# Inverse deviations and exponentials as powers on GpSimd instead of Sqrt and Exp on ScalarE

## The chip, the cores and the metric

One core of a Trainium2 chip runs the whole program. The metric is the device time of one execution in microseconds; the profile adds a span, from the first to the last instruction. The engines are TensorE (PE), VectorE (DVE), ScalarE (ACT), GpSimd (POOL) and SyncE (SP); each works through its own queue in order, and they meet through semaphores.

## The reference

The input x is 32 images of 64 channels, 16 x 16 pixels, fp32. Two blocks with residuals are computed. The second one, which the change touches, is a layer norm over 64 channels, a softmax router over 8 experts with the top two kept, and a mixture of expert networks:

```python
x = x + _L0_conv_ref(_ln_c(x), L0_conv_w)          # fake-quantised 3x3 convolution
t = _to_tokens(x)
t = t + _L0_ffn_ref(_ln_t(t), gate_w, gate_b, W1, b1, W2, b2)

def _ln_t(v, eps=1e-05):
    return (v - mean(v)) / sqrt(var(v) + eps)

logits = xf @ gate_w + gate_b
probs = softmax(logits)
top2_vals, top2_idx = top_k(probs, 2)              # cw: these two values at their experts, else 0
# over the 8 experts:
h = gelu(xf @ w1 + bb1);  y = h @ w2 + bb2;  acc = acc + cw_e * y
```

## The kernel before

The 32 images are handled as 16 pairs: two images of 64 channels fill the 128 partitions, and their 4096 columns are cut into 8 chunks of W = 512. A chunk holds 1024 tokens, as 8 groups of 128 (GROUPS). The order of work on every engine is written out by hand; an engine runs its queue in order.

Stage 1 (to about 35 us) is the first norm and the fake quantisation of its result. Stage 2 (35 to 57 us): TensorE convolves chunk c (convolve, L885), and two chunks behind subtracts the channel means of the new x by a product with a centering matrix (center_x2). GpSimd writes each quantised chunk into a padded tile (quantised, L337) and adds the residual of chunks 0 to 4 (residual, L345); its queue is quantised(0), (1), (2), residual(0), quantised(3), residual(1), then for c = 4, 5, 6 quantised(c) and residual(c-2), and quantised(7).

The second norm: ScalarE squares the centered chunk (square, L386), VectorE sums by group (reduce_squares, L563), ScalarE takes sqrt(sum/64 + eps) for a part of several chunks (deviations, L391), VectorE inverts it (invert, L569) and multiplies (normalise, L575). The parts are chunks 0-1, 2-3 and 4-7 (LN2_PARTS): 16, 16 and 32 columns for a partition.

The router: TensorE transposes the normalised chunk (transpose_x2), a copy brings it to SBUF (take_xT), and TensorE takes the logits. VectorE adds the bias, takes the maximum over experts and subtracts it (shifted_logits, L688, semaphore z_ready). ScalarE takes exponentials in place in ex (exponentials, L455, semaphore exp_ready); the parts are again chunks 0-1, 2-3 and 4-7 (LOGIT_PARTS), 128, 128 and 256 columns. For each chunk VectorE then finds the top two: route_copy (L703, to lcur), route_max, route_index, route_sum (L723, waits for exp_ready), route_select, and route_gates (L733), which multiplies exponentials, selection and inverse sum. TensorE transposes the gates (transpose_gates, L933), ScalarE copies them (take_gateT), and SyncE writes them to DRAM and reads them back spread over the partitions (spread_gates, L250).

Stage 3 (69 us to the end) is the expert networks, 8 units (experts) for each of 8 chunks. A unit is first_product (L947, weights times tokens), Gelu on ScalarE (gelus, L487), second_product (L960), weigh on VectorE (L744: bias, times gate, into y_sb, a ring of 4 tiles), and add_unit on GpSimd (L363: add y to x2). TensorE's first product may run two units ahead of the Gelu; second_product(n) waits for weighted >= n-1, and weigh(n) waits until add_unit(n-4) is done. Inside ffn on VectorE (L757) the router of chunk c+2 is spread between the weigh steps; in ffn(0) shifted_logits(2) stands after weigh(0,3), and route_gates(2) after weigh(0,4).

ScalarE holds one table of functions at a time. Square and Copy need no load of their own in this trace; the loads are for Sqrt (start), Exp (L459, twice) and Gelu (L500 and L504, each a dummy activation that draws the load forward). exponentials(2) stands after the 8 Gelus of chunk 0.

Of the kernel before, what the change touches and what calls it, by code (L numbers as in the profile page):

```python
# [3 lines left out]


IMAGES, CH, SIDE = 32, 64, 16
PIX = SIDE * SIDE
EXPERTS, HIDDEN = 8, 128
TAPS = 9
PAIRS = IMAGES // 2  # L10
NCH = 8
# [3 lines left out]
GROUPS = 2 * TILES  # L15
# [5 lines left out]
LN1_EPS, LN2_EPS = 1e-6, 1e-5  # L21
# [25 lines left out]
def program(nc, x, conv_w, gate_w, gate_b, W1, b1, W2, b2, out):  # L47
# [15 lines left out]
    with ctx:  # L63
        def sb(name, shape, dt=fp32):
            return ctx.enter_context(nc.sbuf_tensor(name, shape, dt))
# [15 lines left out]

        logit = sb("logit", [128, NCH, GROUPS, EXPERTS])
        lmax = sb("lmax", [128, NCH, GROUPS])
        ex = sb("ex", [128, NCH, GROUPS, EXPERTS])
        lcur = sb("lcur", [128, GROUPS, EXPERTS])
        top = sb("top", [128, GROUPS, 8])
        topi = sb("topi", [128, GROUPS, 8], u32)
# [93 lines left out]
        ss2 = sem("ss2")  # L181
# [102 lines left out]
        def _(pool):  # L284
            count = [0]

            def link(ins):
                count[0] += 1
                ins.then_inc(pool_link, 1)
                pool.wait_ge(pool_link, count[0])  # L290
# [3 lines left out]

            pool.memset(center[:, :], 0.0)
            pool.memset(gate_bd[:, :, :], 0.0).then_inc(gatebd_zero, 1)
            link(pool.memset(identf[:, :], 0.0))
            pool.memset(center[0:CH, 0:CH], -1.0 / CH)
            link(pool.memset(center[CH:128, CH:128], -1.0 / CH))
# [37 lines left out]
            def quantised(c):  # L337

                wait_alone(pool, (biased_ready, c + 1))
                pool.tensor_tensor(qpad[:, ds(2 * c, 2), 1:SIDE + 1, 1:SIDE + 1],  # L340
                                   work[:, ds(c * W, W)].rearrange("p (q h w) -> p q h w", q=2, h=SIDE),
                                   xn[:, ds(c * W, W)].rearrange("p (q h w) -> p q h w", q=2, h=SIDE),
                                   ALU.subtract).then_inc(q_ready, 1)

            def residual(c):  # L345

                wait_alone(pool, (conv_taken, c + 1))
                pool.tensor_tensor(x2[:, ds(c * W, W)], x2[:, ds(c * W, W)], x_sb[:, ds(c * W, W)],  # L348
                                   ALU.add).then_inc(x2_ready, 1)

            quantised(0)
            quantised(1)
            quantised(2)
# [1 line left out]
            quantised(3)  # L355
            residual(1)

            with pool.Fori(4, NCH - 1) as c:
                quantised(c)
                residual(c - 2)  # L360
            quantised(NCH - 1)

            def add_unit(c, u):  # L363
                n = UNITS * c + u
# [7 lines left out]

            for u in range(UNITS):
                add_unit(0, u)
            with pool.Fori(1, NCH - 1) as c:
                for u in range(UNITS):
                    add_unit(c, u)
# [5 lines left out]
        def _(act):  # L383
# [68 lines left out]
                act.wait_ge(x2T_ready, c + 1)  # L452
                act.activation(xT[:, ds(c * W, W)], bank(c), ACT.Copy).then_inc(xT_by_act, 1)  # L453

            def exponentials(k):  # L455

                first, last = LOGIT_PARTS[k]
                act.wait_ge(z_ready, k + 1)
                act.activation(ex[:, first:last, :, :], ex[:, first:last, :, :], ACT.Exp).then_inc(exp_ready, 1)  # L459

            def take_gateT(c):

                act.wait_ge(gateT_done, c + 1)
# [4 lines left out]
                               ACT.Copy).then_inc(gateT_ready, 1)  # L468


            deviations(LN2_PARTS[0], ss2, eps2, std2)
            square(3, cent2, sq2)
            deviations(LN2_PARTS[1], ss2, eps2, std2)
            square(4, cent2, sq2)
            square(5, cent2, sq2)
            take_xT(0)
            square(6, cent2, sq2)
            take_xT(1)
            square(7, cent2, sq2)
            deviations(LN2_PARTS[2], ss2, eps2, std2)  # L480
            exponentials(0)
            take_xT(2)
            take_xT(3)
            take_gateT(0)
            exponentials(1)

            def gelus(c, gates_after=2):  # L487
                for u in range(UNITS):
# [10 lines left out]

            act.activation(std[:, 0, 0:1], eps1[:, 0:1], ACT.Gelu)  # L500
            gelus(0, gates_after=3)
            exponentials(2)

            act.activation(std[:, 0, 0:1], eps1[:, 0:1], ACT.Gelu)  # L504
            with act.Fori(1, NCH - 1) as c:
                gelus(c)
            gelus(NCH - 1, gates_after=None)
# [2 lines left out]
        def _(dve):  # L510
# [177 lines left out]
            def shifted_logits(k):  # L688

                first, last = LOGIT_PARTS[k]  # L690
                n = (last - first) * GROUPS
                at = logits_at(first)
                dve.wait_ge(logits_done, last)
                l = logit[:, first:last, :, :].rearrange("p z g e -> p (z g) e")
                link(dve.tensor_tensor(l, ps[:, at:at + n * EXPERTS].rearrange("p (g e) -> p g e", e=EXPERTS),
                                       gb_sb[:, :].unsqueeze(1).to_broadcast([128, n, EXPERTS]), ALU.add))
                m = lmax[:, first:last, :].rearrange("p z g -> p (z g)")
                link(dve.tensor_reduce(m, l, AX.X, ALU.max))
                dve.tensor_tensor(ex[:, first:last, :, :].rearrange("p z g e -> p (z g) e"), l,
                                  m.unsqueeze(2).to_broadcast([128, n, EXPERTS]), ALU.subtract).then_inc(z_ready, 1)  # L700


# [74 lines left out]

            reduce_squares(2, sq2, ss2)
            residual(5)
            invert(LN2_PARTS, 0, std2, rstd2)  # L780
            normalise(0, LN2_PARTS, rstd2, xn2_ready)
            normalise(1, LN2_PARTS, rstd2, xn2_ready)
            reduce_squares(3, sq2, ss2)
            residual(6)
            invert(LN2_PARTS, 1, std2, rstd2)
            normalise(2, LN2_PARTS, rstd2, xn2_ready)
            normalise(3, LN2_PARTS, rstd2, xn2_ready)
            residual(7)
# [5 lines left out]
            shifted_logits(0)  # L794
            settled()
            route_copy(0)
            invert(LN2_PARTS, 2, std2, rstd2)
            route_max(range(GROUPS))
            normalise(4, LN2_PARTS, rstd2, xn2_ready)
            route_index(range(GROUPS))  # L800
# [231 lines left out]
```

## Time and profile before

| | us |
|---|---|
| median of 3 runs | 219.78 |
| their lowest and highest | 218.99, 220.37 |
| the profiled execution | 218.63 |
| its span, first to last instruction | 216.7 |

| engine | busy us | share of the span |
|---|---|---|
| PE (matmul) | 188.4 | 87% |
| DVE | 137.1 | 63% |
| POOL | 115.5 | 53% |
| ACT | 104.8 | 48% |

Busy shares are averages over three stages of different kinds. A matmul's end is modelled, so TensorE's share says that it seldom lacks work and not that it is at its peak. A bracket at the end of a row, as [0.28 <-ACT work L494], gives the engine's idle time just before the instruction and what ended it. TensorE's granted clock is a share of full speed: 1.00 is 2.4 GHz, 0.50 is 1.2 GHz.

### The profile page before, as it was taken

To read this page: it belongs to the slowest core of one execution; us is meant where nothing else is said; L and a number is where in the kernel's file an instruction comes from. 1 tells how busy PE (TensorE), PEld (TensorE's weight loads), DVE (VectorE), ACT (ScalarE), POOL (GpSimd) and SP (SyncE) were. 2 spreads that over 40 slices of the span, in tenths; PEclk is the share of its full clock that TensorE was granted. 3 is DMA by queue.
4 is the path that set the end of the run, shared out by engine and by line. 5 is a ranking of instruction groups with operands and counts; after the bars stand their busy time and mean duration, and the time that the engine had idled before them with its cause. 6 is when DMAs were issued, how large, how long until landed. Compare 5 with 4: busy or idle time off the path is not lost.

```text
span 216.7 us, 3237 instructions
## 1 busy us (share of the span) xinstructions
PE 188.4 (87%) x859; PEld 73.1 (34%) x859; DVE 137.1 (63%) x436; ACT 104.8 (48%) x140; POOL 115.5 (53%) x108
## 2 busy tenths in 40 slices
PE   2966105999979989999999999999999999999990
PEld 2954101566766335422222222222222222222220
DVE  0999999996759655754754664663773763334342
ACT  2539700333372724396465555645555465554640
POOL 7696007799000024456565665756656565665663
PEclk9999755999995899999999999999999999999998
DMA  6940000000000593970890890693692593495101
GB/s 175 316 71 3 0 2 0 0 3 0 3 0 1 142 201 79 202 166 7 209 224 11 203 213 28 152 204 88 166 206 67 143 207 91 124 200 120 50 0 48
DMA packets 16176, 22.36 MB, mean 103 GB/s; under 512 B 2202, under 2 KB 7970, under 8 KB 16162
## 3 DMA queue, kind: packets, MB, share of 16 engines
q1 hardware_dynamic: 16002, 22.04, 45.0%
q8 instruction: 7, 0.11, 0.2%
q10 hardware_dynamic: 160, 0.15, 0.2%
q14 instruction: 7, 0.06, 0.1%
HBM read 19.82 MB, written 2.36 MB: 102 GB/s over the span
## 4 chain that ended last, share of the span: by engine, by line
PE 74%; DVE 14%; issue 4%; DMA 2%; ACT 2%; POOL 1%; POOLq 1%; DVEq 1%; ACTq 0%
PE ps L956 30%; PE ps L971 27%; PE ps L889 8%; PE ps L846 3%; PE ps L929 3%; DVE ssum L566 2%; DVE xn L578 2%; DMA cw<-in_conv_w 2%; PE ps L916 2%; DVE topi L715 1%; DVE gbc L613 1%; PE ps L944 1%; DVE xn L617 1%; DVE cw_x L601 1%; DVE cw_max L539 1%
## 5 line engine op out<-in xcount | busy, mean ns | idle before, releaser
L370 POOL TENSOR_TENSOR x<-x,y_sb 128x512 f32 (+1 forms) x63 | 80.2, 1272 | 79.2 <-DVE y_sb L754 79.1
L494 ACT ACTIVATE work<-ps,bias_sb 128x1024 f32<-128x1024 f32 x64 | 71.2, 1114 | 62.9 <-PE ps L956 62.9
L754 DVE SCALAR_TENSOR_TENSOR y_sb<-ps,bias_sb,gbc 128x512 f32<-128x512 f32 x64 | 48.0, 750 | 59.4 <-PE ps L971 56.5
L956 PE MATMUL ps<-xT,w_sb 64*128 64x512 f32 x256 | 73.4, 650 | 0.1
L971 PE MATMUL ps<-work,w_sb 128*64 128x512 f32 x256 | 68.8, 617 | 0.1
L956 PEld LDWEIGHTS ps<-xT,w_sb 64*128 64x128 f32 x256 | 19.6, 188 | 43.4 <-issue 42.4
L971 PEld LDWEIGHTS ps<-work,w_sb 128*64 128x64 f32 x256 | 12.8, 134 | 48.5 <-issue 37.7
L889 PE MATMUL ps<-qpad,cw_bd 128*128 128x512 bf16 x72 | 18.6, 410 | 10.2 <-POOL qpad L340 10.2
L340 POOL TENSOR_TENSOR qpad<-work,xn 128x512 bf16<-128x512 f32 (+1 forms) x8 | 11.1, 1401 | 7.4 <-issue 7.4
L389 ACT ACTIVATE work<-ps 128x512 f32<-128x512 f32 x16 | 9.3, 596 | 10.9 <-PE ps L846 10.9
L889 PEld LDWEIGHTS ps<-qpad,cw_bd 128*128 128x128 bf16 x72 | 7.2, 101 | 19.4 <-issue 12.6
L846 PE MATMUL ps<-center,x_sb 128*128 128x128 f32 x64 | 9.1, 313 | 3.8 <-DMA x_sb<-in_x 3.8
L566 DVE TENSOR_REDUCE ssum<-work 128x8 f32<-128x512 f32 x16 | 10.5, 678 | 2.6 <-ACT work L389 2.6
L442 ACT ACTIVATE x<-ps 128x512 f32<-128x512 f32 x5 | 3.0, 599 | 18.2 <-PE ps L889 18.2
L929 PE MATMUL ps<-gate_bd,xT 128*128 128x16 f32 x64 | 9.0, 284 | 1.4 <-ACT xT L453 1.4
L846 PEld LDWEIGHTS ps<-center,x_sb 128*128 128x128 f32 x64 | 8.9, 228 | 3.8 <-POOL stack_id L306 3.8
L929 PEld LDWEIGHTS ps<-gate_bd,xT 128*128 128x128 f32 x64 | 8.7, 218 | 3.3 <-ACT xT L453 1.7
L578 DVE TENSOR_TENSOR xn<-ps,rstd 128x512 f32<-128x512 f32 x14 | 9.2, 682 | 0.1
L715 DVE FIND_INDEX8 topi<-top,lcur 128x8 uint32<-128x8 f32 x64 | 8.9, 159 | 0.0
L348 POOL TENSOR_TENSOR x<-x,x_sb (+1 forms) x5 | 7.8, 1564 | 1.6 <-ACT x L442 1.6
L846 PEld LDWEIGHTS ps<-center,x 128*128 128x128 f32 x64 | 8.2, 191 | 1.0
L846 PE MATMUL ps<-center,x 128*128 128x128 f32 x64 | 8.4, 275 | 0.0
(88 smaller groups left out, 140.3 us busy)
## 6 DMA issues: line engine op xcount, KB each, us to landing
gbc<-gate_rows SPq DMA_DIRECT2D x16, 768.0 KB, 9.7
gbc<-gate_rows SPq DMA_DIRECT2D x16, 256.0 KB, 4.1
x_sb<-in_x SPq DMA_DIRECT2D x8, 256.0 KB, 5.5
out<-x SPq DMA_DIRECT2D x8, 256.0 KB, 9.7
w_sb<-in_W SPq DMA_DIRECT2D x3, 256.0 KB, 6.9
gate_rows<-gateT SPq DMA_DIRECT2D x8, 32.0 KB, 1.9
cw<-in_conv_w ACTq DMA_DIRECT2D x2, 72.0 KB, 3.7
gate_bd<-in_gate_w SPq DMA_DIRECT2D x2, 2.0 KB, 6.1
```

What stands on the lines that cost most here:

```text
L340: pool.tensor_tensor(qpad[:, ds(2 * c, 2), 1:SIDE + 1, 1:SIDE + 1], work[:, ds(c * W, W)].rearrange("p (q h w) -> p q h w", q=2, h=SIDE), ...
L370: pool.tensor_tensor(x2[:, ds(c * W, W)], x2[:, ds(c * W, W)], y_sb[:, u % H_RING, :], ALU.add).then_inc(added, 1)
L494: act.activation(h_sb[:, u % H_RING, :], bank(H + 2 * (u % 2), 2 * W), ACT.Gelu, bias=b1_sb[:, u:u + 1]).then_inc(gelu_done, 1)
L566: dve.tensor_reduce(ssum[:, ds(c, 1), :].rearrange("p z g -> p (z g)"), by_group(work[:, ds(c * W, W)]), AX.X, ALU.add).then_inc(summed, 1)
L578: dve.tensor_tensor(by_group(xn[:, ds(c * W, W)]), by_group(bank(c)), wide_groups(rstd, c), ALU.mult).then_inc(ready, 1)
L715: last = dve.max_index(topi[:, g, :], top[:, g, :], lcur[:, g, :])
L754: dve.scalar_tensor_tensor(y_sb[:, u % H_RING, :], bank(Y + u % 2), b2_sb[:, u:u + 1], gbc[:, slot, u, :], ALU.add, ALU.mult).then_inc(wei ...
L846: last = pe.matmul(ps[:, col:col + 128], src[:, col:col + 128], center[:, :], start=True, stop=True)
L889: last = pe.matmul(bank(c), cw_bd[:, k, :, :].rearrange("p r o -> p (r o)"), qpad[:, ds(2 * c, 2), k // 3:k // 3 + SIDE, k % 3:k % 3 + SID ...
L929: last = pe.matmul(by_image[:, :, t, :], xT[:, c * W + t * 128:c * W + (t + 1) * 128], gate_bd[:, :, :], start=True, stop=True)
L956: last = pe.matmul(bank(H + 2 * (u % 2) + r), w1_sb[r * CH:(r + 1) * CH, u * HIDDEN:(u + 1) * HIDDEN], xT[r * CH:(r + 1) * CH, ds(c * W, W ...
L971: last = pe.matmul(ps[r * CH:(r + 1) * CH, (Y + u % 2) * W:(Y + u % 2 + 1) * W], w2_sb[:, u, :], h_sb[:, u % H_RING, r * W:(r + 1) * W], s ...
```

## The change

The Sqrt activations of the second norm and VectorE's three reciprocals behind them are replaced by (ssum/64 + eps) to the power -0.5 on GpSimd: one tensor_scalar and one tensor_tensor with the operation pow. The router's Exp becomes e to the power z, one tensor_tensor on GpSimd for each part; VectorE writes the shifted logits into a new tile z instead of ex. Two constant tiles are filled at the start (256 and 32 columns). GpSimd's loop over c = 4 to 6 is written out, so that inverse_deviations(0) can stand between residual(3) and quantised(6). inverse_deviations(1) and (2) and exponentials(0) and (1) follow quantised(7); exponentials(2) stands after add_unit(0,3). ScalarE loses the Exp table loads and the second Gelu load with its dummy.

```diff
@@ gpsimd
+            pool.memset(euler[:, :], math.e)
+            pool.memset(neg_half[:, :], -0.5)
...
+            def inverse_deviations(k):
+                first, last = LN2_PARTS[k]
+                n = (last - first) * GROUPS
+                wait_alone(pool, (ss2, last))
+                link(pool.tensor_scalar(std[:, first:last, :], ssum[:, first:last, :], 1.0 / CH, LN2_EPS,
+                                        ALU.mult, ALU.add))
+                pool.tensor_tensor(rstd[:, first:last, :].rearrange("p z g -> p (z g)"),
+                                   std[:, first:last, :].rearrange("p z g -> p (z g)"),
+                                   neg_half[:, 0:n], ALU.pow).then_inc(rstd2, 1)
+            def exponentials(k):
+                first, last = LOGIT_PARTS[k]
+                n = (last - first) * GROUPS * EXPERTS
+                wait_alone(pool, (z_ready, k + 1))
+                pool.tensor_tensor(ex[:, first:last, :, :].rearrange("p z g e -> p (z g e)"), euler[:, 0:n],
+                                   z[:, first:last, :, :].rearrange("p z g e -> p (z g e)"),
+                                   ALU.pow).then_inc(exp_ready, 1)
...
-            with pool.Fori(4, NCH - 1) as c:
+            for c in range(4, NCH - 1):
                 quantised(c)
                 residual(c - 2)
+                if c == 5:
+                    inverse_deviations(0)
             quantised(NCH - 1)
+            inverse_deviations(1)
+            inverse_deviations(2)
+            exponentials(0)
+            exponentials(1)
...
             for u in range(UNITS):
                 add_unit(0, u)
+                if u == 3:
+                    exponentials(2)
@@ scalar
-            deviations(LN2_PARTS[0], ss2, eps2, std2)
             square(3, cent2, sq2)
-            deviations(LN2_PARTS[1], ss2, eps2, std2)
...
-            deviations(LN2_PARTS[2], ss2, eps2, std2)
-            exponentials(0)
             take_xT(2)
             take_xT(3)
             take_gateT(0)
-            exponentials(1)
...
             act.activation(std[:, 0, 0:1], eps1[:, 0:1], ACT.Gelu)
             gelus(0, gates_after=3)
-            exponentials(2)
-
-            act.activation(std[:, 0, 0:1], eps1[:, 0:1], ACT.Gelu)
@@ vector
-                dve.tensor_tensor(ex[:, first:last, :, :].rearrange("p z g e -> p (z g) e"), l,
+                dve.tensor_tensor(z[:, first:last, :, :].rearrange("p z g e -> p (z g) e"), l,
...
-            invert(LN2_PARTS, 0, std2, rstd2)
...
-            invert(LN2_PARTS, 1, std2, rstd2)
...
-            invert(LN2_PARTS, 2, std2, rstd2)
```

## Rows read from the trace of the kernel before

**Rows 1.** The page's head and its first part: span, busy time by engine.
```profile
span 216.7 us, 3237 instructions
PE 188.4 (87%) x859; PEld 73.1 (34%) x859; DVE 137.1 (63%) x436; ACT 104.8 (48%) x140; POOL 115.5 (53%) x108
```

**Rows 2.** The chain that ended last: start us, us, what.
```profile
52.37 2.02 PE ps L889 x9
...
68.06 0.28 DVE gate L741
68.39 0.42 PE ps L944
...
76.54 0.28 DVE gate L741
```

**Rows 3.** Timeline of ScalarE, 92 to 96 us: start us, us, instruction.
```profile
92.48 1.28 ACT L459 ACT_TABLE_LOAD   x1
...
94.21 1.28 ACT L504 ACT_TABLE_LOAD   x1
```

**Rows 4.** Timeline of TensorE, 92 to 97 us (PEld is its weight load).
```profile
92.23 1.13 PE L956 MATMUL ps<-xT,w_sb 64*128 64x512 f32 x4
...
94.30 1.13 PE L956 MATMUL ps<-xT,w_sb 64*128 64x512 f32 x4
...
96.76 0.30 PEld L956 LDWEIGHTS ps<-xT,w_sb 64*128 64x128 f32 x4 [0.28 <-ACT work L494]
```

**Rows 5.** GpSimd's instructions by line and form: busy us, mean ns.
```profile
L318 POOL TENSOR_SCALAR gbc<-gbc 128x288 f32<-128x288 f32 x4 | 4.8, 1212 | 1.8 <-DVE gbc L547 1.7
...
L321 POOL TENSOR_TENSOR gbc<-gbc 128x864 f32<-128x864 f32 x1 | 2.0, 2014 | 0.1
L323 POOL TENSOR_TENSOR gbc<-gbc 128x288 f32<-128x288 f32 x1 | 0.8, 797 | 0.1
```

**Rows 6.** Timeline of VectorE: reciprocals and subtractions of two sizes.
```profile
52.12 0.24 DVE L573 RECIPROCAL rstd<-std 128x16 f32<-128x16 f32 x1
...
63.74 0.29 DVE L699 TENSOR_TENSOR ex<-logit,lmax 128x128 f32<-128x128 f32 x1
...
64.05 0.34 DVE L573 RECIPROCAL rstd<-std 128x32 f32<-128x32 f32 x1
...
89.12 0.42 DVE L699 TENSOR_TENSOR ex<-logit,lmax 128x256 f32<-128x256 f32 x1
```

**Rows 7.** Timeline of GpSimd beside VectorE: where both work at once.
```profile
41.20 1.45 POOL L340 TENSOR_TENSOR qpad<-work,xn 128x512 bf16<-128x512 f32 x1
41.45 1.24 DVE L622 TENSOR_SCALAR gbc<-gbc 128x32 f32<-128x32 f32 x1
...
91.17 1.27 POOL L370 TENSOR_TENSOR x<-x,y_sb 128x512 f32<-128x512 f32 x1 [2.52 <-DVE y_sb L754]
...
91.27 1.25 DVE L737 TENSOR_TENSOR picked<-ex,sel 128x64 f32<-128x64 f32 x1
```

**Rows 8.** Timeline of GpSimd around 50 us: quantised(6).
```profile
50.18 1.26 POOL L340 TENSOR_TENSOR qpad<-work,xn  x1
```

**Rows 9.** Timeline of VectorE: route_sum(0), and z of the second part.
```profile
66.50 0.20 DVE L726 TENSOR_REDUCE esum<-ex 128x8 f32<-128x64 f32 x1
...
69.45 0.29 DVE L699 TENSOR_TENSOR ex<-logit,lmax 128x128 f32<-128x128 f32 x1
```

**Rows 10.** Timeline of VectorE: route_copy(1) and take_xT(4).
```profile
70.25 0.18 DVE L704 COPY lcur<-logit 128x64 f32<-128x64 f32 x1
...
71.91 0.69 DVE L686 COPY xT<-ps 128x512 f32<-128x512 f32 x1 [1.47 <-PE ps L916]
```

**Rows 11.** Timeline of VectorE and TensorE: weigh(0,5) and second_product(0,7).
```profile
92.70 0.75 DVE L754 SCALAR_TENSOR_TENSOR y_sb<-ps,bias_sb,gbc 128x512 f32<-128x512 f32 x1
...
95.36 1.08 PE L971 MATMUL ps<-work,w_sb 128*64 128x512 f32 x4
```

**Rows 12.** Windows of the span: busy time by engine, then TensorE's clock (PEclk), DMA.
```profile
71.00:72.00 1.00, 1.00 (x6) 0.67 (x7) 0.09 (x1) 0.99 (x3) 0.00 (x0) 0.50 0.00 0
72.00:73.00 1.00, 1.00 (x4) 0.28 (x4) 1.00 (x9) 0.60 (x1) 0.00 (x0) 0.90 0.12 47
```

More of the change, by code:

```diff
@@ L3 @@
 from contextlib import ExitStack
+import math
 IMAGES, CH, SIDE = 32, 64, 16
@@ L83, in program @@
         lmax = sb("lmax", [128, NCH, GROUPS])
+        z = sb("z", [128, NCH, GROUPS, EXPERTS])
         ex = sb("ex", [128, NCH, GROUPS, EXPERTS])
+        euler = sb("euler", [128, 4 * GROUPS * EXPERTS])
+        neg_half = sb("neg_half", [128, 4 * GROUPS])
         lcur = sb("lcur", [128, GROUPS, EXPERTS])
@@ L453, in take_xT @@
                 act.activation(xT[:, ds(c * W, W)], bank(c), ACT.Copy).then_inc(xT_by_act, 1)
[L455 to L459, printed above, removed]
             def take_gateT(c):
```

## The prediction

> **What bounds the kernel now.** The page comes first: TensorE is busy 87% of a span of 216.7 us, ScalarE 48%, GpSimd 53% [rows 1]. The profiled execution took 218.63 us, so 1.93 us lie outside the span; it is 1.15 us under the median of the runs shown (219.78), and the sum below is a difference that I add to the median. The busy shares say that ScalarE has room on the average, so the next view is the chain that ended last. From 76.54 us on it is TensorE's own products almost without a break; before that, between 63 and 77 us, it runs through the router on VectorE: the gates of chunk 0 end at 68.34 and TensorE transposes them at 68.39, the gates of chunk 1 follow at 76.54 [rows 2]. So there are two stretches to price: 50 to 77 us, where the second norm and the router sit, and 88 to 98 us, where exponentials(2) sits.
>
> **What is removed from ScalarE.** After gelus(0) ScalarE loads the Exp table (1.28 us), takes the exponentials and loads Gelu again (1.28 us) [rows 3]; with both activations it is away for 3.1 us. That looks like 3.1 us in the chain. But TensorE runs two products ahead: first products start at 92.23 and 94.30, 2.07 apart, and the next at 96.76, 2.46 apart, with 0.28 us of waiting for ScalarE [rows 4]. Part of the 0.39 is the gate transpose, which stands here in every chunk, so both loads together cost TensorE some 0.2 us. I take -0.2 us. The Exp load at 62.6 us and the Sqrt activations are also gone, but the copies that they delay (take_xT(2) and (3), then logits(2) and (3)) feed the logits of chunks 2 and 3, and those end (68.1) before VectorE has chunk 0's gates: worth nothing. VectorE loses three reciprocals; the last, 0.34 us long at 64.05 [rows 6], lies in the router's chain and overlaps what follows it: -0.25 us.
>
> **What a power costs.** No row of before has one. Floor: an add of GpSimd. Its tensor_tensor takes 2014 ns for 864 columns and 797 ns for 288, so 2.1 ns a column and 0.17 us fixed [rows 5]. A power can't be cheaper: 0.20, 0.24, 0.45 and 0.72 us for 16, 32, 128 and 256 columns. For more than a floor I have only the one row group of an iterated function: VectorE's reciprocal grows from 0.24 to 0.34 us for 16 more columns, 6.3 ns a column, where its two-input subtract grows from 0.29 to 0.42 for 128 more, 1.0 a column [rows 6]. So one such function is about 6 simple passes, 13 ns a column at GpSimd's rate, and a power holds two (a logarithm and an exponential): 26 ns a column. That is my estimate; the upper end is twice it, 52. At 26: 0.58 us (16), 1.0 (32), 3.5 (128), 6.8 (256). Its tensor_scalar of two operations is 1212 ns for 288 columns [rows 5], 3.6 ns a column, so 0.23 us for 16, plus 0.08 us for the linked wait.
>
> **The port.** The exponentials' powers also lie beside VectorE's work, and that is no free cover. picked<-ex,sel (two inputs in SBUF, 64 columns) takes 1.25 us at 91.27 [rows 7], where the two-input subtract takes 0.42 for 256 columns [rows 6]: it stands until GpSimd's add, begun at 91.17, has ended at 92.44. The short bound step of 32 columns took 1.24 us at 41.45, beside GpSimd's work of 41.20 to 42.65 [rows 7]. So such a VectorE instruction waits for GpSimd's whole instruction. The Trainium skill has this as a rule (SBUF — State Buffer, Who interferes with whom): the pair of ports is an exclusive lock for the length of an instruction, against VectorE's two-SBUF-input operations and its 2-port modes. By that rule a long power is worse than several short adds; the trace agrees for 1.27 us adds, and shows no longer one. Without the lock the sum would be +1.3 instead of +6.4 (below).
>
> **Step A, inverse_deviations(0).** It goes between residual(3) and quantised(6), which starts at 50.18, ends 51.44 [rows 8]. Its input is there (chunks 0 and 1 are reduced by 49.1). Added 0.05 + 0.23 + 0.08 + 0.58 = 0.94 us; convolve(6) starts 52.37 [rows 2], which leaves 0.93 less some 0.13 for the signal, so 0.8 us are free: +0.15. inverse_deviations(1) is done at 55.9 instead of 55.3, in front of normalise(2) and (3); VectorE has 0.7 us idle before residual(7), which hides that, and without it the delay would be the 0.6. inverse_deviations(2) is done by 63.9, under VectorE's shifted_logits(0) and maxima, where normalise(4) comes at 64.8; uncovered it would cost its 1.4 us. The two constant fills (under 0.5 us) lie before TensorE has its first input at 3.85: nothing.
>
> **Step B, exponentials(0).** z is written at 64.03 (L699, 63.74 + 0.29) [rows 6]. With A, the power runs 64.35 to 67.85. route_sum(0) stood at 66.50 [rows 9] and now starts at 67.95: +1.45 in all, A and the lost reciprocal included. Behind it VectorE's queue holds the selection, normalise(5) and the gates; TensorE is behind its transpose_gates(0), ScalarE and the gate rows' DMAs behind that. Nothing hides it.
>
> **Step C, exponentials(1).** z is ready at 69.74 [rows 9], now 71.2; the power runs 71.3 to 74.8. VectorE's next instruction after normalise(7) is the copy to lcur at 70.25 (SBUF to SBUF, 184 ns for 64 columns), then take_xT(4) at 71.91 [rows 10]. The short copy is of the kind that stood at 41.45, so I let it wait for the power: take_xT(4) starts at 74.9 instead of 73.4, and the whole route(1) with it: +1.5. Its own reader, route_sum(1), would have been served in time.
>
> **Step D, exponentials(2).** z is written at 89.54 (89.12 + 0.42) [rows 6], now 92.5, and GpSimd has finished add_unit(0,3); the power runs until 99.45. VectorE meanwhile reaches route_gates(2), whose first two-input operation stood just ahead of 91.27; it waits for the port. Then picked loses another 1.27 us to add_unit(0,4), as it does today, and weigh(0,5), which was at 92.70 [rows 7, 11], starts 101.1 and ends 101.9. second_product(0,7), at 95.36 [rows 11], wants it, and would come at 98.3 with B and C: +3.6. The ring of four y tiles adds nothing: weigh(1,0) wants add_unit(0,4), done by 101.
>
> **Sum.** 1.45 + 1.5 + 3.6 - 0.2 = +6.4 us (+2.9%): 225.0 on the profiled execution, 226.2 us on the median. As a formula for s ns a column: B = T128 - 2.05, C = T128 - 2.0, D = T256 - 3.2, each at least zero, with T = 0.17 + s times columns. Break-even is at about s = 13.6; +1% at about 18.
>
> **The clock.** TensorE's granted clock is still 0.50 at 71 to 72 us and 0.90 over the next microsecond [rows 12], so it rises at 72.2; it had fallen after an idle stretch at 63.5 to 64.9. In the new kernel TensorE idles longer before the gates, from about 65.4 to 69.8. Half speed through 4 us more of products would cost 2 us, full speed where it is now half would give back up to 1.9. I take 0 and keep this for the range.
>
> **The rivals.** *Cheap power* (not slower): if the power costs less than 13.6 ns a column, steps B, C and D vanish together, the forecast turns, and what is left is -0.2 -0.25: 219.3 us. For it: GpSimd's plain add is only 2.1. Against: a power is no plain operation. *No lock for powers*: if a power that reads SBUF seldom lets VectorE through, C and D are zero (route_sum(1) comes at 76.9, the power ends 74.8; the y ring has over 8 us), B stays: +1.45 - 0.2, 221.0 us. Against: the waits at 91.27 and 41.45 last to the end of the other instruction. *Dearer power*, 52 ns a column: T128 6.8, T256 13.5; A delays convolve(6) by 0.6 and holds up the shifted logits by 0.75, so B becomes 5.9, C 4.9, D 10.3: 240.7 us. *No effect on the tables* can't be: Gelu, Copy and Square are all that is left behind the first norm.
>
> **How the numbers follow.** Forecast (18 to 40 ns, lock) 0.38; dearer 0.18; cheap or nearly (under 18) 0.30; no lock 0.14. A measurement of this kernel can tell about 1% from no change. Slower by over 1%: the forecast, the dearer and 0.04 of the no-lock case, 0.60. Within 1%: 0.25 of the cheap and 0.10 of the no-lock case, 0.35. Faster by over 1% needs 2.2 us, more than all that is removed; only the clock could bring it: 0.05. The range goes from the cheap case with some of the clock's gain, 218.8, to the dearer one, 240.7; the likeliest case by itself is 222 to 233.
>
> **What would show it.** The durations of the powers of 16, 32, 128 and 256 columns; route_sum(0) starting when the first exponentials end; the copy to lcur and the first operation of route_gates(2) stretched to the end of a power; a gap of TensorE before second_product(0,7); no table load after 71 us. I am wrong if the powers' slope is under 14 ns or over 50, if VectorE's two-input operations keep their length beside a power, or if TensorE's clock stays low in the first units by more than now.

## The result and the profile after

The changed kernel takes 287.68 us (median of 4 runs, 287.04 to 288.92) where the one before took 219.38 in the same session: a ratio of 1.313, 95% interval 1.304 to 1.321. That is 68.3 us more by the two medians and 68.6 by the ratio. I had forecast 226.2 us and a range up to 240.7. The direction was right, the size was wrong by a factor of ten, and the time lies 47 us outside the range.

The head of the page of the changed kernel, its first part and the first lines of its chain that ended last (shares of the span by engine, then by line):

```profile
span 285.6 us, 3219 instructions
PE 198.8 (70%) x859; PEld 77.3 (27%) x859; DVE 137.1 (48%) x433; ACT 99.5 (35%) x130; POOL 211.1 (74%) x119
...
PE 46%; POOL 33%; DVE 10%; issue 5%; DMA 2%; DVEq 1%; POOLq 1%; ACT 0%; ACTq 0%
```

Against [rows 1], the span is 68.9 us longer and GpSimd is busy 95.6 us more, while VectorE has the same 137.1 and ScalarE lost 5.3. The chain, in which GpSimd had 1%, now has 33% of it. The six powers are the reason. This is GpSimd's timeline (start us, us, instruction; in brackets the idle time before it):

```profile
51.28 2.96 POOL L364 TENSOR_TENSOR rstd<-std,neg_half 128x16 f32<-128x16 f32 x1
...
66.19 5.43 POOL L364 TENSOR_TENSOR rstd<-std,neg_half 128x32 f32<-128x32 f32 x1
71.58 20.78 POOL L373 TENSOR_TENSOR ex<-euler,z 128x128 f32<-128x128 f32 x1
95.80 20.77 POOL L373 TENSOR_TENSOR ex<-euler,z 128x128 f32<-128x128 f32 x1 [3.44 <-DVE z L719]
...
124.65 41.24 POOL L373 TENSOR_TENSOR ex<-euler,z 128x256 f32<-128x256 f32 x1 [2.53 <-DVE z L719]
165.87 1.26 POOL L402 TENSOR_TENSOR x<-x,y_sb 128x512 f32<-128x512 f32 x1
```

I had priced 16, 32, 128 and 256 columns at 0.58, 1.0, 3.5 and 6.8 us. They take 2.9, 5.4, 20.8 and 41.2: 0.16 us a column, six times my estimate. What waited for them stands in VectorE's timeline:

```profile
92.40 0.22 DVE L746 TENSOR_REDUCE esum<-ex 128x8 f32<-128x64 f32 x1 [18.96 <-POOL ex L373]
...
96.17 0.18 DVE L724 COPY lcur<-logit 128x64 f32<-128x64 f32 x1
...
116.61 0.22 DVE L746 TENSOR_REDUCE esum<-ex 128x8 f32<-128x64 f32 x1 [9.37 <-POOL ex L373]
...
127.87 0.18 DVE L756 TENSOR_TENSOR sel<-sel 128x64 f32<-128x64 f32 x1
128.08 0.23 DVE L757 TENSOR_TENSOR picked<-ex,sel 128x64 f32<-128x64 f32 x1
...
167.26 0.75 DVE L774 SCALAR_TENSOR_TENSOR y_sb<-ps,bias_sb,gbc 128x512 f32<-128x512 f32 x1 [32.13 <-POOL x L402]
```

Three rows carry an idle time: route_sum(0), route_sum(2) and weigh(1,0). The three others say something as important: the copy to lcur, and the two two-input operations of route_gates(2), run beside a power and keep their lengths of 0.18, 0.18 and 0.23 us. Their counterparts for the two later places in the kernel before, which [rows 9] doesn't hold, are (timeline of VectorE, kernel before):

```profile
81.00 0.21 DVE L726 TENSOR_REDUCE esum<-ex 128x8 f32<-128x64 f32 x1
...
98.95 0.75 DVE L754 SCALAR_TENSOR_TENSOR y_sb<-ps,bias_sb,gbc 128x512 f32<-128x512 f32 x1 [1.71 <-PE ps L971]
```

So the 68.9 us can be placed. route_sum(0) is at 92.40 instead of 66.50, +25.9. Of this, z came 3.5 us late (67.55 against 64.03), exponentials(0) stood 4.0 us behind the power of 32 columns in GpSimd's queue, and the power itself is 20.8 less the 2.5 us that lay between z and route_sum(0) anyway. The gates of chunk 1 are at 102.68 instead of 76.54 [rows 2], +26.1, so nothing is added there. route_sum(2) is at 116.61 instead of 81.00, +35.6: exponentials(1) adds 9.5. z of the third part is written at 124.51 instead of 89.54, +35.0, and weigh(1,0) is at 167.26 instead of 98.95, +68.3: exponentials(2) adds 33.3. The last 0.6 us come after it.

Not all of the 3.5 us by which z is late belongs to a power. TensorE's center_x2 just ahead of convolve(6) is already at 52.84 instead of 51.31, 1.5 us late, and at that moment no power has been waited for. About 0.3 of this are the two constant fills (GpSimd's first step in the quantisation of the weights starts at 9.18 instead of 8.88); the rest lies within the 2 us by which executions of the kernel before differ. The deviations' powers thus explain 2.0 us of z's delay and the 4.0 us behind it.

ScalarE's table loads are gone as the diff says: two are left (Sqrt at the start, Gelu at 95.06) of five.

### The profile page after: what moved, and what is told of

Same layout as the page of the kernel before. It is cut to its first block, busy times and chain, and to the rows that moved or that the text cites. A ratio compares the mean times of both kernels' runs of the same rounds, so it can differ in the third digit from the quotient of the medians.

```text
span 285.6 us, 3219 instructions
## 1 busy us (share of the span) xinstructions
PE 198.8 (70%) x859; PEld 77.3 (27%) x859; DVE 137.1 (48%) x433; ACT 99.5 (35%) x130; POOL 211.1 (74%) x119
## 4 chain that ended last, share of the span: by engine, by line
PE 46%; POOL 33%; DVE 10%; issue 5%; DMA 2%; DVEq 1%; POOLq 1%; ACT 0%; ACTq 0%
POOL ex L373 28%; PE ps L988 20%; PE ps L973 20%; PE ps L906 3%; POOL qpad L346 2%; DVE ssum L586 2%; POOL x L354 2%; DVE xn L598 2%; DMA cw<-in_conv_w 2%; PE ps L863 1%; PE ps L946 1%; DVE y_sb L774 1%; POOL x L402 1%; DVE xn L637 1%; DVE gbc L633 1%
## 5 line engine op out<-in xcount | busy, mean ns | idle before, releaser
L988 PE MATMUL ps<-work,w_sb 128*64 128x512 f32 x256 | 72.4, 646 | 34.7 <-DVE y_sb L774 34.6
L373 POOL TENSOR_TENSOR ex<-euler,z 128x128 f32<-128x128 f32 (+1 forms) x3 | 82.8, 27598 | 6.0 <-DVE z L719 6.0
L973 PE MATMUL ps<-xT,w_sb 64*128 64x512 f32 x256 | 76.5, 675 | 0.0
L906 PE MATMUL ps<-qpad,cw_bd 128*128 128x512 bf16 x72 | 19.4, 424 | 11.8 <-POOL qpad L346 11.8
L961 PE MATMUL ps<-identf,gate 128*64 128x128 f32 x8 | 2.5, 314 | 26.0 <-DVE gate L761 26.0
L346 POOL TENSOR_TENSOR qpad<-work,xn 128x512 bf16<-128x512 f32 x8 | 11.7, 1469 | 7.0 <-DVE work L662 7.0
L746 DVE TENSOR_REDUCE esum<-ex 128x8 f32<-128x64 f32 (+1 forms) x8 | 1.7, 212 | 28.3 <-POOL ex L373 28.3
L906 PEld LDWEIGHTS ps<-qpad,cw_bd 128*128 128x128 bf16 x72 | 7.3, 104 | 21.7 <-issue 13.6
L495 ACT ACTIVATE gateT<-ps 64x128 f32<-64x128 f32 x8 | 2.1, 260 | 27.1 <-PE ps L961 27.1
L364 POOL TENSOR_TENSOR rstd<-std,neg_half 128x16 f32<-128x16 f32 (+1 forms) x3 | 11.3, 3767 | 0.2
L863 PEld LDWEIGHTS ps<-center,x_sb 128*128 128x128 f32 x64 | 10.1, 253 | 3.9 <-POOL stack_id L312 3.9
L946 PEld LDWEIGHTS ps<-gate_bd,xT 128*128 128x128 f32 x64 | 9.8, 241 | 2.4 <-issue 2.4
```

What stands on the lines that cost most here:

```text
L373: pool.tensor_tensor(ex[:, first:last, :, :].rearrange("p z g e -> p (z g e)"), euler[:, 0:n], z[:, first:last, :, :].rearrange("p z g e - ...
L863: last = pe.matmul(ps[:, col:col + 128], src[:, col:col + 128], center[:, :], start=True, stop=True)
L906: last = pe.matmul(bank(c), cw_bd[:, k, :, :].rearrange("p r o -> p (r o)"), qpad[:, ds(2 * c, 2), k // 3:k // 3 + SIDE, k % 3:k % 3 + SID ...
L946: last = pe.matmul(by_image[:, :, t, :], xT[:, c * W + t * 128:c * W + (t + 1) * 128], gate_bd[:, :, :], start=True, stop=True)
L973: last = pe.matmul(bank(H + 2 * (u % 2) + r), w1_sb[r * CH:(r + 1) * CH, u * HIDDEN:(u + 1) * HIDDEN], xT[r * CH:(r + 1) * CH, ds(c * W, W ...
L988: last = pe.matmul(ps[r * CH:(r + 1) * CH, (Y + u % 2) * W:(Y + u % 2 + 1) * W], w2_sb[:, u, :], h_sb[:, u % H_RING, r * W:(r + 1) * W], s ...
```

## The experiments

Theory 1, formed from the two traces: the whole loss is the powers' own length, exposed where a queue or a data wait has no cover for it, and a power does not hold VectorE's port. Its rivals: the new order on GpSimd costs by itself; the length of a power depends on the data; the port is held after all.

### Is it the powers alone?

```diff
-                                   ALU.pow).then_inc(exp_ready, 1)
+                                   ALU.mult).then_inc(exp_ready, 1)
```

(and the same in inverse_deviations).

> The changed kernel with the operation pow replaced by mult in its six tensor_tensor instructions: queues, waits, tiles and the written-out loop are those of the changed kernel, the inverse deviations and exponentials are left out (the tiles hold products). Theory 1, the time lies in the powers' own length alone: each of the six is 0.2 to 0.8 us long and the kernel is within 0.5 us of the one before (218.5 to 219.8 us), as my cheap-power case had it. Rival, the new order on GpSimd or the moved waits cost by themselves: slower than before by 2 us or more, with a gap at quantised(6) or at route_sum(0).

Measured: 219.78 us against 219.75 for the kernel before, a ratio of 0.9992, interval 0.996 to 1.0024. GpSimd's timeline in this run:

```profile
64.66 0.46 POOL L373 TENSOR_TENSOR ex<-euler,z 128x128 f32<-128x128 f32 x1 [1.25 <-DVE z L719]
70.35 0.46 POOL L373 TENSOR_TENSOR ex<-euler,z 128x128 f32<-128x128 f32 x1 [5.23 <-DVE z L719]
...
91.21 0.73 POOL L373 TENSOR_TENSOR ex<-euler,z 128x256 f32<-128x256 f32 x1 [0.42 <-DVE z L719]
```

Queues, waits, tiles and the written-out loop are those of the changed kernel, and the 68 us are gone. The rival of the new order falls. The run says something more: with the replacing instructions almost free, the removal of two Exp loads, one Gelu load, seven activations and three reciprocals gives nothing that can be measured. With this order of the queues, the most that the change could have brought was 0 within 0.4%. Whether another placement gains more was not run.

### The exponentials alone, the deviations alone

The changed kernel with one half undone, each time back in the place of the kernel before:

```diff
@@ exponentials as powers, deviations back on ScalarE
-                if c == 5:
-                    inverse_deviations(0)
...
-            inverse_deviations(1)
-            inverse_deviations(2)
...
+            deviations(LN2_PARTS[0], ss2, eps2, std2)
             square(3, cent2, sq2)
...
```

> The changed kernel with the second norm's deviations back on ScalarE (Sqrt) and VectorE (reciprocal); only the exponentials are powers. Theory 1 (0.161 us a column, exposed by the queues): exponentials(0) runs from about 64.2 to 85, route_sum(0) moves from 66.5 to 85 (+18.5); exponentials(1) holds route_sum(2) back by 9 to 10; exponentials(2) holds add_unit(0,4) and through the ring of four y tiles weigh(1,0), +31 to 33. Sum +59 to 61: 278 to 281 us. Rival, the six powers cost by their total length (94 us) times some share and the three of the norm matter as much as the rest: below 270.

```diff
@@ deviations as powers, exponentials back on ScalarE
-            exponentials(0)
-            exponentials(1)
...
-                if u == 3:
-                    exponentials(2)
...
             gelus(0, gates_after=3)
+            exponentials(2)
+            act.activation(std[:, 0, 0:1], eps1[:, 0:1], ACT.Gelu)
...
```

> The changed kernel with the exponentials back on ScalarE (and with them the two Exp loads and the second Gelu load); only the inverse deviations are powers. Theory 1: the power of 16 columns (2.95 us) ahead of quantised(6) delays convolve(6) by 2.5 us, and the one of 32 columns (5.4 us) ends 6 us after the last square sum, so normalise(4) and route_sum(0) come about 7 us late and nothing gives it back: 226 to 227 us. Rival, these three lie hidden as I forecast: within 1 us of before.

Measured: the exponentials alone 281.72 us, ratio 1.2815 (1.274 to 1.289), +61.9; theory 1 had +59 to 61, so it is at the edge. The deviations alone 226.35 us, ratio 1.0297 (1.022 to 1.038), +6.5, as expected, from two executions 3 us apart (224.83 and 227.88). The two add up to 68.4, and the whole change costs 68.6: within the 2 us that these few runs can tell, the halves do not hide each other. In the run with the exponentials alone, the waits (who waited for whom: us in total, times, longest) are these:

```profile
DVE y_sb L773 <- POOL x L398: 32.3, 1, 32.3
DVE esum L745 <- POOL ex L373: 28.1, 2, 18.5
```

They are the same two places as in the changed kernel: route_sum(0) and route_sum(2) with 18.5 and 9.6 us, weigh(1,0) with 32.3. In the run with the deviations alone, TensorE and GpSimd show where the time goes (timeline, then a window of the span as in [rows 12]). The trace is of the slower of the two executions, with a span 9.1 us longer than that of the kernel before:

```profile
50.90 2.96 POOL L364 TENSOR_TENSOR rstd<-std,neg_half 128x16 f32<-128x16 f32 x1
53.84 1.27 POOL L346 TENSOR_TENSOR qpad<-work,xn 128x512 bf16<-128x512 f32 x1
...
55.17 3.80 PE L913 MATMUL ps<-qpad,cw_bd 128*128 128x512 bf16 x9 [2.57 <-POOL qpad L346]
...
67.25 5.43 POOL L364 TENSOR_TENSOR rstd<-std,neg_half 128x32 f32<-128x32 f32 x1
...
55.20:58.50 3.30, 3.30 (x8) 1.10 (x9) 0.58 (x1) 0.00 (x0) 3.13 (x4) 0.50 0.00 0
```

quantised(6) stands behind the first power and convolve(6) waits 2.57 us for it; the nine products then take 3.80 us where the other chunks' took 2.19, because TensorE's granted clock has fallen to its lower level (0.50 in that window). So z of the first part is 4.6 us late. Then the power of 32 columns runs until 72.68, with normalise(4) behind it, and route_sum(0) is 7.9 us late. In the changed kernel's own trace convolve(6) waits less, and its clock stays at 1.00:

```profile
55.55 2.20 PE L906 MATMUL ps<-qpad,cw_bd 128*128 128x512 bf16 x9 [1.66 <-POOL qpad L346]
```

The same power ahead of quantised(6) thus cost 1.66 us in one execution and 2.57 + 1.6 us in the other.

### What a power costs, and of what

Ten instructions at the end of GpSimd's queue, each waited for, on constant tiles:

```diff
+            FORMS = [("tt", 16, math.e, -1.5), ("tt", 64, math.e, -1.5), ("tt", 256, math.e, -1.5),
+                     ("tt", 64, math.e, 0.0), ("tt", 64, 1.0, 1.0), ("tt", 64, 2.0, 3.0), ("tt", 64, 0.7, -0.5),
+                     ("tt", 64, math.e, -30.0), ("add", 64, 0.7, -0.5), ("p32", 64, math.e, -1.5)]
```

> The kernel before with ten more GpSimd instructions on tiles of their own behind its last add, each waited for. Its total says nothing; their durations do. Powers of 16, 64 and 256 columns with base e and exponent -1.5; of 64 columns with exponent 0, with 1 to the power 1, 2 to the power 3, 0.7 to the power -0.5, e to the power -30 (which must leave the ordinary path if special values are cut short or dear); 64 columns on 32 partitions; and an add of 64 columns. Theory 1: 0.4 us plus 0.161 a column whatever the values and the partitions: 3.0, 10.7, 41.6 us, and 0.31 for the add. Rival 2, the length depends on the data: values such as exponent 0 or 1 to the power 1 take another time than 10.7 us.

GpSimd's timeline, in order the powers of 16, 64 and 256 columns, 0.7 to the power -0.5, the add of 64 columns, and the power on 32 partitions:

```profile
215.14 3.43 POOL L392 TENSOR_TENSOR formo<-forma,formb 128x16 f32<-128x16 f32 x1
...
218.94 10.55 POOL L392 TENSOR_TENSOR formo<-forma,formb 128x64 f32<-128x64 f32 x1
...
230.19 41.24 POOL L392 TENSOR_TENSOR formo<-forma,formb 128x256 f32<-128x256 f32 x1
...
304.54 10.54 POOL L392 TENSOR_TENSOR formo<-forma,formb 128x64 f32<-128x64 f32 x1
...
326.37 0.32 POOL L392 TENSOR_TENSOR formo<-forma,formb 128x64 f32<-128x64 f32 x1
...
327.05 10.54 POOL L392 TENSOR_TENSOR formo<-forma,formb 32x64 f32<-32x64 f32 x1
```

(41.24 - 10.55) / 192 = 0.160 us a column and 0.3 us fixed. All five other pairs of values took 10.54 us, 1 to the power 1 and e to the power 0 among them, and 32 partitions cost what 128 do. So among what was varied the length depends on the columns alone, and the rival of the data falls for these six pairs. An add of the same 64 columns is 33 times shorter. Not expected: this first power took 3.43 us, where 16 columns took 2.92 to 2.96 in the changed kernel; why is open.

### Only exponentials(2), and the ring of y tiles

The kernel before, with one power:

```diff
+                if u == 3:
+                    wait_alone(pool, (z_ready, 3))
+                    pool.tensor_tensor(ex[:, 4:8, :, :].rearrange("p z g e -> p (z g e)"), euler[:, :],
+                                       z2[:, :, :, :].rearrange("p z g e -> p (z g e)"),
+                                       ALU.pow).then_inc(exp_ready, 1)
@@ scalar
-            exponentials(2)
-            act.activation(std[:, 0, 0:1], eps1[:, 0:1], ACT.Gelu)
```

(VectorE writes z of the third part into z2.)

> The kernel before, with only exponentials(2) as a power on GpSimd at the place it has in the changed kernel (256 columns, about 41.3 us, after add_unit(0,3)), and its two table loads gone from ScalarE. Theory 1 (the power does not hold VectorE's port; the ring of four y tiles is what stalls): weigh(0,4) to weigh(0,7) run on as before, weigh(1,0) waits for add_unit(0,4), about 132.2 us instead of 98.95: +31 to 33.5, 250 to 253 us. Rival, the port is held for the whole power: the first operation of route_gates(2) stands until 131 and weigh(0,5) behind it, +37 or more: 256 us and above.

And the same with eight y tiles (y_sb, its index and weigh's wait on added; the ring of h stays at four):

```diff
-                    dve.wait_ge(added, n - H_RING + 1)
+                    dve.wait_ge(added, n - Y_RING + 1)
```

> As the kernel with only exponentials(2) on GpSimd, with a ring of eight y tiles in place of four. Theory 1: weigh(1,4) is the first to wait for add_unit(0,4), four units of 2.07 us later than weigh(1,0), so the stall is 8.3 us shorter: 242 to 245 us. Rival, what stalls is the port or TensorE's wait for something else: no difference from the ring of four.

Measured: 253.59 us with four tiles, ratio 1.1557 (1.149 to 1.162), +34.2, just above theory 1's 31 to 33.5 and short of the rival's 37; 245.45 us with eight, ratio 1.1186 (1.112 to 1.125), +26.0. The difference is 8.1 us where four units of 2.07 us make 8.3. Timeline of VectorE and GpSimd with four tiles:

```profile
91.20 41.30 POOL L381 TENSOR_TENSOR ex<-euler,z 128x256 f32<-128x256 f32 x1 [0.43 <-DVE z L706]
...
92.48 0.17 DVE L743 TENSOR_TENSOR sel<-sel 128x64 f32<-128x64 f32 x1
92.69 0.23 DVE L744 TENSOR_TENSOR picked<-ex,sel 128x64 f32<-128x64 f32 x1
...
97.91 0.75 DVE L761 SCALAR_TENSOR_TENSOR y_sb<-ps,bias_sb,gbc 128x512 f32<-128x512 f32 x1 [1.32 <-PE ps L978]
133.88 0.75 DVE L761 SCALAR_TENSOR_TENSOR y_sb<-ps,bias_sb,gbc 128x512 f32<-128x512 f32 x1 [35.22 <-POOL x L374]
```

weigh(0,4) to weigh(0,7) run on in the 2.07 us step beside the power; the next one waits 35 us for add_unit(0,4), which stands behind the power. With eight tiles, the last weigh ahead of the gap is four units further on:

```profile
107.05 0.75 DVE L762 SCALAR_TENSOR_TENSOR y_sb<-ps,bias_sb,gbc 128x512 f32<-128x512 f32 x1 [0.22 <-PE ps L979]
...
134.39 0.75 DVE L762 SCALAR_TENSOR_TENSOR y_sb<-ps,bias_sb,gbc 128x512 f32<-128x512 f32 x1 [26.32 <-POOL x L375]
```

So the ring is what turns a late GpSimd into a stalled TensorE, and the port is not. From z to weigh(1,0) it is 42.82 us (91.06 to 133.88) where it was 9.41 (89.54 to 98.95): the power of 41.30 us costs 33.4, and 7.9 are covered. In the changed kernel the same reckoning gives 33.3 of 41.24. Nobody reads these exponentials before route_sum(4), two chunks later: the stall is a matter of the queue they stand in.

### How much of a power the ring covers

The kernel before with an added power of 96 or 48 columns on tiles of its own at the same place; ScalarE keeps its loads.

```diff
+                if u == 3:
+                    wait_alone(pool, (z_ready, 3))
+                    pool.tensor_tensor(junk[:, :], junk_a[:, :], junk_a[:, :], ALU.pow)
```

> The kernel before with a power of 96 columns on tiles of its own after add_unit(0,3), 15.7 us long (0.3 + 0.160 a column); both table loads stay. Theory 1, in numbers from the run of exponentials(2) alone (41.3 us long, +34 us): the ring of four y tiles and TensorE's lead together cover about 7 us of a GpSimd stall at this place, so this one costs 15.7 - 7 = 8.7 us: 227.5 to 229 us. Rival, the stall is proportional to the power's length (34/41 of it): +13 us, 232 to 233.

> As the one before with 48 columns, 8.0 us long. Theory 1: 8.0 - 7 = 1 us, +0.5 to +1.5 us (220 to 221). Rival, proportional: +6.6 us, 226.

Measured: 227.94 us for 96 columns, ratio 1.0368 (1.033 to 1.041), +8.1; 220.34 for 48, ratio 1.0008 (0.997 to 1.004), nothing that shows. The proportional rival (+13 and +6.6) falls. The cover is a little more than the 7 us that I took: 15.7 - 8.1 = 7.6 us, from 96 columns. The expected +0.5 to +1.5 of the 8 us power was at the edge of what the runs can tell, and they do not show it. The traces say it more closely. This is weigh(1,0) with 96 and with 48 columns:

```profile
107.46 0.75 DVE L760 SCALAR_TENSOR_TENSOR y_sb<-ps,bias_sb,gbc 128x512 f32<-128x512 f32 x1 [9.51 <-POOL x L373]
...
100.00 0.75 DVE L760 SCALAR_TENSOR_TENSOR y_sb<-ps,bias_sb,gbc 128x512 f32<-128x512 f32 x1 [1.90 <-POOL x L373]
```

z of the third part was written at 90.25 and 90.40, so from there to weigh(1,0) it is 17.21 and 9.60 us against 9.41 in the kernel before: +7.8 for a power of 15.68 us and +0.2 for one of 8.06. The cover is 7.9 us in both, as with the power of 41.30.

### The port

The same place again, once with an add of 2048 columns and once with a power of 28, both a few microseconds long. The input tile is filled at the start of GpSimd's queue, and it has as many columns as the instruction:

```diff
-                    pool.tensor_tensor(junk[:, :], junk_a[:, :], junk_a[:, :], ALU.pow)
+                    pool.tensor_tensor(junk[:, :], junk_a[:, :], junk_a[:, :], ALU.add)
```

> The kernel before, with one more instruction on GpSimd after add_unit(0,3), begun when z of the third part is written as the power is in the changed kernel: an add of 2048 columns on tiles of its own, about 4.5 us long. By the rule of the port lock VectorE's first two-input operation of route_gates(2) (about 91.1 us) stands until the add ends (94.2), weigh(0,5) comes 3 us late where TensorE has 1.9 us to spare: +1 to +1.5 us, and the operation shows about 3 us where it took 0.17.

> As the run with the added add, with a power of 28 columns in its place, about 4.9 us long, on tiles of its own. Theory 1: the power lets VectorE's two-input operations through, they take 0.17 and 0.23 us beside it, add_unit(0,4) comes 3.4 us late and the ring takes that up: no change of the time (within 0.3 us). Rival, the port is held by any GpSimd instruction that reads SBUF: +1 to +1.5 us as with the add.

Measured: with the add 221.92 us, ratio 1.0103 (1.005 to 1.016), +2.3; with the power 220.0, ratio 1.002 (0.9985 to 1.005). Timeline of GpSimd and VectorE beside the add:

```profile
92.82 3.60 POOL L380 TENSOR_TENSOR junk<-junk_a 128x2048 f32<-128x2048 f32 x1 [1.21 <-DVE ex L705]
...
94.20 2.30 DVE L742 TENSOR_TENSOR sel<-sel 128x64 f32<-128x64 f32 x1
...
96.38 1.28 POOL L373 TENSOR_TENSOR x<-x,y_sb 128x512 f32<-128x512 f32 x1
...
96.54 1.20 DVE L743 TENSOR_TENSOR picked<-ex,sel 128x64 f32<-128x64 f32 x1
```

In the same trace, the fill of the input tile, z of the third part, and second_product(0,7), which waits for weigh(0,5):

```profile
0.97 1.80 POOL L299 MEMSET junk_a<- 128x2048 f32 x1
...
92.25 0.42 DVE L705 TENSOR_TENSOR ex<-logit,lmax 128x256 f32<-128x256 f32 x1
...
98.80 1.08 PE L977 MATMUL ps<-work,w_sb 128*64 128x512 f32 x4 [0.24 <-DVE y_sb L760]
```

And beside the power:

```profile
89.58 4.84 POOL L380 TENSOR_TENSOR junk<-junk_a 128x28 f32<-128x28 f32 x1 [0.89 <-DVE ex L705]
...
90.95 0.17 DVE L742 TENSOR_TENSOR sel<-sel 128x64 f32<-128x64 f32 x1
...
91.16 0.22 DVE L743 TENSOR_TENSOR picked<-ex,sel 128x64 f32<-128x64 f32 x1
91.42 0.28 DVE L747 TENSOR_TENSOR gate<-picked,rsum 128x64 f32<-128x64 f32 x1
```

Beside the add, the selection's sum (0.17 us alone) stands 2.30 us, to the add's end at 96.42. Beside the power, which is longer, it takes its 0.17, and picked even avoids the wait that it has today, since add_unit(0,4) comes later.

The +2.3 us are not the price of this wait. The fill of 2048 columns takes 1.80 us at the start (that of 28 columns 0.12), and TensorE's first convolution starts at 36.82 instead of 35.10. z of the third part, after which the add starts, is at 92.67 instead of 89.54: 3.1 of the 3.3 us by which this trace's span is longer lie ahead of the add. From z on, weigh(0,5) comes 2.1 us later than in the kernel before (5.24 us behind z against 3.16), TensorE waits 0.24 us for it, and the first product of the next chunk starts 7.37 us behind z, where it is 7.22 in the kernel before and beside the power. So the port costs TensorE about 0.15 us here, not the +1 to +1.5 that I expected; the 1.9 us that TensorE has to spare take up nearly all of it, and the add was shorter than I had reckoned (3.60 against 4.5 us). What the two runs compare cleanly is the length of VectorE's operation, and not the total.

The short copy to lcur, which takes 0.18 us beside a power, is held up by adds too: it takes 0.55 us in this run with the power of 28 columns (99.50, beside an add_unit of 98.73 to 100.00), and 0.69 in the run with only exponentials(2) (134.54, beside one that ends at 135.18).

## Why the prediction was wrong

**The price of a power: wrong, and the largest term.** I had 26 ns a column, with 52 as the upper end; it is 160. The floor came from a row of GpSimd, the rest from an analogy: VectorE's reciprocal costs six simple passes, so a power is two such. Nothing in the trace of before tied GpSimd's power to VectorE's reciprocal, and a bound "twice the estimate" bounded nothing. From GpSimd's own add at 2.1 ns a column to the measured 160 is a factor of 76, and none of the rows named for it lay in between. The dearer rival was right in its direction, and its slope too was a third of the truth. At 0.160 us a column my formula would have given 18.8 + 18.8 + 38.1 - 0.2, about +75 us. That this comes near the measured 68 would have been luck: two of its three large terms are waits that did not take place, and step A is missing from it.

Two small slips in the working change nothing. The add's fixed part is 797 - 288 x 2.1 ns, or 0.19 us and not 0.17. And B, C and D do not vanish together at 13.6 ns: by their formulas B ends below 14.7, C below 14.3 and D only below 11.8.

**Step A: mechanism right, size by the price.** The 0.8 us of freedom before convolve(6) fits one trace: 2.96 + 0.20 + 0.13 less 0.8 is 2.5, and TensorE waits 2.57 in the run with the deviations alone. In the changed kernel it waits 1.66, so there the freedom was about 1.6; how far GpSimd is ahead of TensorE differs between executions by nearly 1 us. The constant fills, which I put at nothing, are not hidden: the two of the change delay GpSimd by 0.3 us, and the fill of 1.80 us in the run with the add delays the first convolution by 1.7. That the two other deviations lie hidden was wrong at this price. The power of 32 columns ends at 71.62 in the changed kernel, and both normalise(4) and exponentials(0) stand behind it.

**Step B: right.** route_sum(0) starts as the first exponentials end. With 20.8 us in my formula, T128 - 2.05 gives 18.75; the run with the exponentials alone has an idle time of 18.5.

**Step C: wrong in its mechanism, by the port.** I let the copy to lcur stand until the power's end. It took 0.18 us beside it. The loss of 9.5 us is another wait, which the prediction did not have: route_sum(2) reads the second part. I had written that route_sum(1) is its reader; chunks 0 and 1 are both in the first part, as the parts in the kernel say, and that sentence was a misreading. By the formula, T128 - 2.0, step C would have been 18.8 at this price.

**Step D: the place right, the mechanism wrong.** I had weigh(0,5) late behind the port, and wrote that the ring adds nothing. The ring is all of it: 33.3 us in the changed kernel, and 8.1 of 34.2 us less with four more tiles. My formula, T256 - 3.2, would give 38.1. The no-lock rival had the port right in C and D, and the ring in D (its cover "over 8 us", measured 7.9); for C it named the same wrong reader. It got 0.14.

**The port's rule.** The Trainium skill (SBUF — State Buffer, Who interferes with whom) says that a VectorE instruction with two SBUF inputs contends with any GpSimd instruction that reads SBUF, and that the shared pair is locked for the whole instruction. For the add the runs agree, 2.30 us to the end of a 3.60 us add. For the power they do not: 0.17, 0.22 and 0.28 us beside 4.84. The measurement decides. The trace of before could only show adds, and I carried them over to an instruction of another kind. Whether a power holds the port for short moments, and how its reads are done, was not tried.

**The gain.** -0.2 us for the loads and -0.25 for the reciprocals were small terms, and the run with mult shows that their sum isn't distinguishable from zero (-0.2 us, interval -0.9 to +0.5). The reading of the first products' starts [rows 4], that 3.1 us of loads in the chain cost TensorE only some 0.2, is borne out by it. Without the loads, these first products, with the gate transpose between them, start 2.29 us apart where it was 2.46 (TensorE in the run with mult), so the loads cost 0.17 us:

```profile
94.91 1.13 PE L973 MATMUL ps<-xT,w_sb 64*128 64x512 f32 x4
...
97.20 1.13 PE L973 MATMUL ps<-xT,w_sb 64*128 64x512 f32 x4
```

**The clock.** I took zero for it. TensorE's clock after the changed kernel's gaps (windows: us, busy time of PE, PEld, DVE, ACT, POOL, then the granted clock, DMA share and GB/s):

```profile
117.00:121.00 4.00, 3.37 (x11) 1.79 (x12) 3.90 (x29) 0.00 (x0) 3.49 (x4) 0.50 1.08 207
...
166.00:172.00 6.00, 3.84 (x8) 0.83 (x8) 4.54 (x29) 0.00 (x0) 5.21 (x5) 0.50 0.00 0
...
174.00:180.00 6.00, 6.00 (x24) 1.35 (x24) 5.46 (x9) 2.98 (x3) 4.60 (x5) 1.00 0.00 0
```

It is at 0.50 (1.2 GHz) when work resumes after each gap and at 1.00 from 174 us. Between weigh(1,0) and the end only 0.6 us are lost in all, so zero was close enough there. It is not zero everywhere: in the run with the deviations alone the lower clock after the wait of 2.57 us makes convolve(6) 1.6 us longer, while after 1.66 us of waiting in the changed kernel the clock stays at 1.00.

## What to carry to other kernels

An operation that no row shows has no price until one is measured: an analogy from another engine missed by a factor of six here, and the honest upper end would have been far wider. Before moving work off an engine to spare it table loads, look at how long the bound engine really waits for that engine: 3.1 us in the chain of waits were 0.2 us of TensorE's time, and even free replacements brought nothing. In a queue with a ring behind it, a long instruction costs its length less what the ring covers (here 7.9 us with four tiles, some 8 more with eight), even if nobody needs its result yet. And a test instruction brings its own preparation along: the fill of a test tile cost more here than the effect that the run was to price, so measure from the nearest event ahead of the change, and not by the total alone.

## What the runs showed of the hardware

- A power on GpSimd (tensor_tensor, fp32) takes 0.3 us and 0.160 us a column, for each of the six pairs of values tried and whether 32 or 128 partitions take part; an add of 64 columns takes 0.32 us, a power 10.54.
- A power does not hold up VectorE's two-input operations or its short copy (0.17 to 0.28 us beside powers of 4.84 to 41.24 us), where an add holds a two-input operation until its own end (2.30 us), and a copy beside adds takes 0.55 to 0.69 us.
- An add of 2048 columns with one tile as both inputs took 3.60 us, 1.7 ns a column; with two inputs of different places it was 2.1 [rows 5]; the two also differ in length, and the cause was not tried.
- TensorE's granted clock fell from 1.00 (2.4 GHz) to 0.50 (1.2 GHz) after a wait of 2.57 us in one trace (nine products 3.80 us instead of 2.19), and stayed at 1.00 after one of 1.66 us at the same place in another.
